# Finer order of norms and maxima, and the PSUM banks of the attentions split three to one

## The reference, cut to what matters

```
x = x + tanh(g_xattn[0]) * differential_attention(q=layernorm(x), k,v=ctx)   # 32 half heads of 8
x = x + tanh(g_ffn[0])   * zone_ffn(layernorm(x))                            # top 3 of 8 zones per sample
x = x + tanh(g_xattn[1]) * cross_attention(q=layernorm(x), k,v=ctx)          # 16 heads of 16
x = x + tanh(g_ffn[1])   * gated_ffn(layernorm(x))                           # silu(gate) * up, hidden 768

layernorm: (x - mean) / sqrt(var + 1e-5)
attention: softmax over the 77 context rows; differential: softmax_even - lam * softmax_odd
zone_ffn:  router from the mean over 1024 rows; sum of w_e * gelu(x @ Wa[e]) @ Wb[e]; plus x
```

## Time and profile before

| what | us |
|---|---|
| median of three runs (762.97 to 767.08) | 765.22 |
| the profiled execution, its own time | 768.97 |
| its span in the profile | 767.2 |
| PE busy in the span | 665.0 (87%) |
| DVE, ACT, POOL busy | 402.6, 337.8, 93.2 |
| mean granted TensorE clock | 0.899 |

### The profile page before, as it was taken

How to read it: one execution, slowest core, us unless ns; L and a number is a source line. 1 busy time by engine, 2 the same in 40 slices (tenths; PEclk the granted TensorE clock), 3 DMA queues, 4 the chain that set the end, 5 groups by cost and what they waited for, 6 DMA issues and landing times.

```text
span 767.2 us, 9986 instructions
## 1 busy us (share of the span) xinstructions
PE 665.0 (87%) x3644; PEld 496.5 (65%) x3644; DVE 402.6 (52%) x870; ACT 337.8 (44%) x555; POOL 93.2 (12%) x114
## 2 busy tenths in 40 slices
PE   1777886797888899999989999998887878999996
PEld 0545453453536778888867888876556666788885
DVE  6666755657677453333445635534445655444332
ACT  2221443454595474655635635543543344222232
POOL 4100123133363000000000000000021123000000
PEclk9956688879798999999999999999887569899999
DMA  6412011101021203030022150000162000000000
GB/s 195 88 25 69 1 43 45 39 25 25 3 84 53 85 1 111 0 110 1 4 107 69 42 165 3 0 1 3 38 171 61 24 3 1 1 1 27 29 29 27
DMA packets 22737, 34.66 MB, mean 45 GB/s; under 512 B 4640, under 2 KB 13216, under 8 KB 22688
## 3 DMA queue, kind: packets, MB, share of 16 engines
q1 hardware_dynamic: 21952, 33.66, 14.9%
q0 software_dynamic: 448, 0.29, 0.4%
q10 hardware_dynamic: 288, 0.07, 0.0%
HBM read 18.93 MB, written 2.10 MB: 27 GB/s over the span
## 4 chain that ended last, share of the span: by engine, by line
PE 74%; DVE 13%; issue 5%; ACT 3%; SPq 2%; POOL 2%; DMA 1%; ACTq 0%; DVEq 0%; POOLq 0%
PE SC L1084 27%; PE PV L1084 22%; PE AUX L1084 6%; PE AUX L1183 5%; PE PV L1102 5%; PE SC L1208 4%; PE AUX L1142 3%; DVE NM L972 3%; DVE XN L899 2%; DVE O L980 1%; DVE ST L879 1%; SPq L502 1%; POOL RSTD L571 1%; DVE QG L802 1%; PE AUX L1194 1%
## 5 line engine op out<-in xcount | busy, mean ns | idle before, releaser
L811 DVE TENSOR_TENSOR HL<-HF,HH 128x512 fp32r<-128x512 f32 x120 | 82.9, 690 | 153.5 <-ACT HH L762 153.2
L722 ACT ACTIVATE PB<-SC 77x1024 f32<-77x1024 f32 x96 | 94.6, 1015 | 73.5 <-PE SC L1208 73.2
L1183 PE MATMUL AUX<-KA,QG 96*128 96x308 f32 (+1 forms) x256 | 79.5, 385 | 37.3 <-DVE NM L972 26.6
L972 DVE TENSOR_REDUCE NM<-AUX 128x4 f32<-128x308 f32 x192 | 85.7, 468 | 38.5 <-PE AUX L1183 36.8
L1183 PEld LDWEIGHTS AUX<-KA,QG 96*128 96x128 f32 x256 | 53.4, 228 | 77.9 <-DVE NM L972 44.3
L762 ACT ACTIVATE HH<-PV 128x512 fp32r<-128x512 f32 x96 | 57.4, 597 | 73.3 <-PE SC L1084 73.2
L757 ACT ACTIVATE HF<-PV 128x512 f32<-128x512 f32 x96 | 57.4, 598 | 58.8 <-PE PV L1084 56.0
L1084 PE MATMUL PV<-XH,WAH 128*128 128x512 f32 x192 | 79.1, 412 | 1.8 <-DVE O L980 1.8
L1084 PE MATMUL PV<-XH,WAL 128*128 128x512 f32 x192 | 76.6, 399 | 0.0
L1084 PE MATMUL PV<-XL,WAH 128*128 128x512 f32 x192 | 76.6, 399 | 0.0
L1084 PE MATMUL SC<-HH,WBH 128*128 128x512 f32 x192 | 76.1, 396 | 0.0
(11 more groups left out here) (177 smaller groups left out, 1155.3 us busy)
## 6 DMA issues: line engine op xcount, KB each, us to landing
QG<-QH SPq DMA_DIRECT2D x128, 64.0 KB, 2.0
WSA<-in_wa SPq DMA_DIRECT2D x6, 1024.0 KB, 4.9
WSB<-in_wb SPq DMA_DIRECT2D x12, 512.0 KB, 6.9
QG<-QL SPq DMA_DIRECT2D x64, 64.0 KB, 2.0
X<-in_x SPq DMA_DIRECT2D x4, 512.0 KB, 6.0
out_x<-X SPq DMA_DIRECT2D x4, 512.0 KB, 2.7
WI<-in_wg SPq DMA_DIRECT2D x1, 768.0 KB, 5.4
WI<-in_wu SPq DMA_DIRECT2D x1, 768.0 KB, 8.8
```

The lines of the kernel that those rows point to most:

```text
L722: act.activation(probs(n)[0:S, :, :], SC[0:S, n % 2, :, :], ACT.Exp, scale=SCALE[a]).then_inc(exp_done, 1)
L811: return dve.tensor_tensor(dst, raw, hi.bitcast(F32), ALU.subtract)
L972: dve.tensor_reduce(NM[:, n % 2, t, 4 * u:4 * u + 4], bank(key)[:, 0:4 * S].rearrange("p (h n) -> p h n", h=4), AX_X, ALU.max, negate=True ...
L1183: ins = pe.matmul(ps[:, i * n_cols:(i + 1) * n_cols], QG[n % 2][0:ROWS, g, P * t:P * (t + 1)], KA[a][0:ROWS, j // 2, NS[a] * g:NS[a] * (g ...
```

## The change: what it does

1. **Norms**: `norm` becomes four `stats` steps and one `norm` step, placed in different gaps; `scale` is a step of its own in the plan, moved to ScalarE (four Identity activations with scale and bias); POOL makes one more small product for its bias. `residual` moves to POOL (two small and four 128x256 instructions).
2. **Maxima**: the heads' halves c = 0 and 1 are handed over apart: `negmax` of one half transposes half the heads, and SP issues 4 DMAs. Attends of the first half wait for the first hand-over only. Of tile 0, half 0 stays in the prologue; half 1 (16 maxima) becomes filler of attention tile 0.
3. **Keys** of the second attention become five steps inside attention tile 1, with the splits of its weights, whose low parts POOL makes (three instructions).
4. **Banks**: outside of zones and gated, one PV bank joins the AUX ring (three slots); `values` use the other bank alone and wait for the `outputs` just before.

```diff
+    def half_maxima(a, j, c):
+        half = units(a) // 2
+        return [("max", a, j, t, c * half + u) for t in range(TT) for u in range(half)] + [("negmax", a, j, c)]
+    def norm(stage, j):
+        return [("stats", stage, j, t) for t in range(TT)] + [("norm", stage, j)]
+    def norm_in(side, at, stage, j, gap, turn_gap):
+        for i, step in enumerate(norm(stage, j)):
+            side.setdefault(at + i // 2, []).append(step)
+        side.setdefault(at + 2 + gap, []).append(("scale", stage, j))
+        side.setdefault(at + 2 + gap + turn_gap, []).append(("turn", stage, j))
-    steps += [("keys", 0)]
-    steps += weave(maxima(0, 0), {3: [("norm", ATT0, 1)], 9: [("turn", ATT0, 1)],
-                                  13: [("query", 0, 1)] + moves(0, 1), 26: [("weights_split", 2)]})
-    steps += [("coefficients",), ("keys", 1)]
+    steps += keys(0, 0, 5) + [("heads", 0)]
+    steps += weave(half_maxima(0, 0, 0), {2: norm(ATT0, 1), 5: [("scale", ATT0, 1)], 8: [("turn", ATT0, 1)],
+                                          11: [("query", 0, 1)] + moves(0, 1)})
+    steps += [("coefficients",)]
...
+        if j == 0:
+            filler = half_maxima(0, 0, 1) + filler
+        if j == 1:
+            side.setdefault(1, []).append(("weights_split", 2))
+            for i, step in enumerate(keys(1, 0, 5)):
+                side.setdefault(6 + 2 * i, []).append(step)
         if j + 2 < J:
-            side.setdefault(1, []).append(("norm", ATT0, j + 2))
-            side.setdefault(3, []).append(("turn", ATT0, j + 2))
-            side.setdefault(6, []).append(("query", 0, j + 2))
+            norm_in(side, 0, ATT0, j + 2, 2, 2)
+            side.setdefault(8, []).append(("query", 0, j + 2))
         if j:
-            side.setdefault(7, []).append(("norm", FFN0, j - 1))
-            side.setdefault(11, []).append(("turn", FFN0, j - 1))
+            norm_in(side, 8, FFN0, j - 1, 2, 2)
-        steps += attention_tile(0, j, side, filler, 0, 12, left)
+        steps += attention_tile(0, j, side, filler, 0, 14 if j else 16, left)
...
-    side.setdefault(3, []).append(("norm", FFN0, 3))
-    side.setdefault(5, []).append(("turn", FFN0, 3))
-    side.setdefault(7, []).append(("residual", 3))
+    side.setdefault(1, []).extend(norm(FFN0, 3))
+    side.setdefault(3, []).append(("scale", FFN0, 3))
+    side.setdefault(5, []).extend([("turn", FFN0, 3), ("residual", 3)])
-    side.setdefault(b1 + 4, []).append(("norm", ATT1, 0))
-    side.setdefault(b1 + 6, []).append(("turn", ATT1, 0))
+    norm_in(side, b1 + 2, ATT1, 0, 1, 2)
+    norm_in(side, b1 + 8, ATT1, 1, 1, 2)
-    side.setdefault(b1 + 44, []).append(("norm", ATT1, 2))
-    side.setdefault(b1 + 46, []).append(("turn", ATT1, 2))
+    side.setdefault(b1 + 43, []).extend(norm(ATT1, 2))
+    side.setdefault(b1 + 45, []).append(("scale", ATT1, 2))
+    side.setdefault(b1 + 47, []).append(("turn", ATT1, 2))
...
-    steps += [("norm", FFN1, 2)]
-    side = {1: [("turn", FFN1, 2)], 3: [("turn_mix", 3)], 5: [("project", 3)], 6: [("norm", FFN1, 3)],
-            10: [("turn", FFN1, 3)]}
+    steps += norm(FFN1, 2)
+    side = {0: [("scale", FFN1, 2)], 1: [("turn", FFN1, 2)], 3: [("turn_mix", 3)], 5: [("project", 3)],
+            6: norm(FFN1, 3), 8: [("scale", FFN1, 3)], 10: [("turn", FFN1, 3)]}
...
+        if step[0] in ("zone", "gated"):
+            banks = 2
+        elif step == ("attend", 1, 0, 0):
+            banks = 3
         for key in slots_of(step):
             aux[key] = len(aux)
+            turn_now = (turn_now + 1) % banks
+            home[key] = (turn_now, uses[turn_now])
...
         def bank(key):
-            return AUX[:, aux[key] % 2, :]
+            n = home[key][0]
+            return AUX[:, n, :] if n < 2 else PV[:, 1, :]
@@ POOL @@
                     pool.tensor_tensor(RSTD[:, 1, :], RSTD[:, 0, :], NHALF[:, :], ALU.pow).then_inc(pool_step, 1)
                     chain += 1
                     pool.wait_ge(pool_step, chain)
+                    pool.tensor_tensor(RSTD[:, 3, :], RSTD[:, 2, :], RSTD[:, 1, :], ALU.mult).then_inc(rstd_ready, 1)
+                elif kind == "residual":
...
                     for t in range(TT):
+                        xt = X[:, TT * j + t, :]
+                        ins = pool.tensor_scalar(xt, xt, AB[:, 0, t:t + 1], AB[:, 1, t:t + 1], ALU.mult, ALU.add)
...
+                elif kind == "weights_split" and step[1] == 2:
+                    pool.wait_ge(split_hi, 5)
+                    lo_part(WQ1L[:, :, :], WQ1R[:, :, :], WQ1H[:, :, :]).then_inc(split1_done, 1)
+                    pool.wait_ge(split_hi, 6)
+                    for c in range(KC):
+                        lo_part(WDL[:, c, :, :, :], ...
@@ ACT @@
+                elif kind == "scale":
+                    _, stage, j = step
+                    n = order[step]
+                    act.wait_ge(rstd_ready, n + 1)
+                    if n:
+                        filled(act, ("turn",) + NORMS[n - 1][1:] + (KC - 1,))
+                    for t in range(TT):
+                        ins = act.activation(XN[:, t, :], X[:, TT * j + t, :], ident_f, scale=RSTD[:, 1, t:t + 1],
+                                             bias=RSTD[:, 3, t:t + 1])
@@ PE @@
-                if q >= 2:
-                    pe.wait_ge(pv_out, q - 1)
+                if q >= 1:
+                    pe.wait_ge(pv_out, q)
...
-                            ins = pe.matmul(PV[32 * r:32 * r + DV + 1, q % 2, at_h:...
+                            ins = pe.matmul(PV[32 * r:32 * r + DV + 1, 0, at_h:...
...
-                    if u == 0:
-                        pe.wait_ge(m_moved[m % 2], 16 * G * (m // 2 + 1))
+                    if u % (units[a] // KC) == 0:
+                        pe.wait_ge(m_moved[m % 2][u // (units[a] // KC)], 16 * (G // KC) * (m // 2 + 1))
```

More of the change, by code:

```diff
@@ L52 @@
 SMALL = 13
-SCALE_LAG = 3
 LAG = 2
@@ L223, in plan @@
     steps += [("gated_end",), ("evac", FFN1, 3), ("out", FFN1, 3)]
-    placed, waiting = [], []
-    for step in steps:
-        if waiting and (step == ("turn",) + waiting[0][1:] or waiting[1] == 0):
-            placed.append(waiting[0])
-            waiting = []
-        placed.append(step)
-        if step[0] == "norm":
-            waiting = [("scale",) + step[1:], SCALE_LAG]
-        elif waiting:
-            waiting[1] -= 1
-    return placed
+    return steps
 def slots_of(step):
@@ L863, in _ @@
                     lo_part(WVL[:, :, :], WVR[:, :, :], WVH[:, :, :]).then_inc(split_done, 1)
+                elif kind == "stats":
+                    _, stage, j, t = step
+                    if t == 0:
+                        if stage == ATT0:
+                            dve.wait_ge(x_in[j], 16)
+                        elif stage == FFN0:
+                            dve.wait_ge(mixed, oct_of(0, j + 1, 0))
+                        else:
+                            for i in range(2):
+                                used(dve, ("out", FFN0, j, i) if stage == ATT1 else ("project", j, i))
+                    ins = dve.bn_stats(ST[:, t, :], X[:, TT * j + t, :])
+                    if t == TT - 1:
+                        ins.then_inc(stats_done, 1)
                 elif kind == "norm":
@@ new lines, in _ @@
+                elif kind == "keys" and step[2] < 3:
+                    _, a, i = step
+                    low = slice(64, ROWS)
+                    key = step + (0,)
+                    groups = range(3 * i, min(3 * i + 3, G))
+                    dve.wait_ge(keys_hi, 3 * a + i + 1)
+                    if a == 0:
+                        kt = KT[0][low, groups[0]:groups[-1] + 1, :]
+                        ins = lo_part(kt, bank(key)[low, 0:len(groups) * B * S].rearrange("p (g n) -> p g n", n=B * S), kt)
+                    else:
+                        for g in groups:
+                            kt = KT[1][low, g, :]
+                            at_g = (g - 3 * i) * B * S
+                            ins = dve.scalar_tensor_tensor(kt, bank(key)[low, at_g:at_g + B * S], BQD[low, g:g + 1],
+                                                           kt.bitcast(F32), ALU.add, ALU.subtract)
+                    ins.then_inc(frees(key), 1)
+                elif kind == "keys":
+                    _, a, i = step
+                    key = step + (0,)
+                    if i == 3:
+                        dve.wait_ge(pool_set, 5)
+                        if a == 1:
+                            dve.wait_ge(small_in, 16 * SMALL)
+                    filled(dve, key)
+                    v = V[a][0:S, i - 3, :, 0:DV]
+                    ps = bank(key)[0:S, 0:D].rearrange("p (h d) -> p h d", d=DV)
@@ L968, in _ @@
                     key = step + (0,)
[L969 to L970 removed]
+                    half = units[a] // 4
+                    if t == 0 and u % half == 0 and n >= 2:
+                        filled(dve, ("negmax", (n - 2) // J, (n - 2) % J, u // half, 0))
                     filled(dve, key)
```

281 lines of the change are left out of this document (117 added, 164 removed).

## The result

The changed kernel took 742.8 us, median of four runs (732.87 to 744.41), the kernel before beside it 764.1: ratio 0.964, 95% interval 0.953 to 0.976. The forecast was 745. Six more runs on another occasion had a median of 738.7 (732.6 to 749.2), ratio 0.965 (0.9605 to 0.970). The profiled run after took 744.27 us, the one before 768.97: 24.7 apart.

What follows compares the result with a forecast made beforehand. The prediction took TensorE, busy 87% of the span, to bound the kernel, so gains had to come from its waits or clock. Terms by stretch, plus the clock, summed to -20.4 from 765.2: 745 us, range 725 to 759.

Steps and rivals of the forecast that it cites:

- Prologue, -6: Before the first attend: work leaves, but SP's query moves ahead of the maxima's DMAs limit the gain to 6 us.
- The ring, two thirds of its waits: Attention tiles 0 to 2: a third AUX bank removes two thirds of the 16.4 us that maxima's matmuls wait.
- Tile 0, +1.9: First attention's tile 0: 16 maxima added, +7.4; DMA stop, ring waits and norm block saved; net 1.9 us longer.
- Tile 1, +0.9: First attention's tile 1: five keys steps cost 6 us, ring waits save 4.8, with smaller terms; net 0.9 us longer.
- Tile 2, -3.8: First attention's tile 2: ring waits -3.4, DMA and norm block -1.4, negmax +1; net 3.8 us shorter.
- Tile 3, +3: First attention's tile 3: ScalarE's extra instructions and the single values bank cost, the moved residual saves; net 3 us longer.
- Clock, -4: Attention tiles 0 to 2: fewer stops raise TensorE's granted clock, saving 4 us; bounds +4 to -18.
- Zones, -6.7: Zones: turns stand further from their norms, so three waits for XN, 8.1 us, go; net 6.7 us shorter.
- D: Rival, chance 0.08: `values` steps wait for transpositions in the single values bank; 24 us or more, 769 us and above.
- A: Rival, chance 0.20: the clock comes back, tiles 0 to 2 run at 0.95; 730 us.
- B: Rival, chance 0.16: finer order makes new waits, the ring saves one third, the clock nothing; 756 us.
- C: Rival, chance 0.06: zones and gated keep their waits in another place, scale standing behind gelus on ScalarE; no change.

Runs made afterwards that it cites:

- e3: The changed kernel with tile 1's 24 query moves placed behind the maxima's four DMAs of tile 0's first half; 732.3 us, ratio 0.960.
- e1: The kernel before with only the ring of three banks and one bank for the values; 753.6 us, ratio 0.984.
- e2: The changed kernel without its ring: two AUX banks and two banks for the values; 762.8 us, ratio 0.9957.
- e4: The changed kernel with the second attention's weight split and keys back ahead of the first attend; 722.2 us, ratio 0.944.
- the second profile: Another profiled run of the changed kernel, nothing changed, also called "again"; 737.92 us.
- e8: The changed kernel with the ring's third bank given back to the values in tile 3 of the first attention; 737.3 us, ratio 0.962.
- e10: The changed kernel with keys and earlier split before the first attend, moves later, two values banks in tile 3, route later, XN on VectorE; 709.8 us, ratio 0.930.
- e11: As e10, but XN written by ScalarE as in the changed kernel; 716.2 us, ratio 0.935.
- e7: The changed kernel with the second attention's split and keys ahead of the first attend and tile 1's query moves behind the maxima's DMAs; 727.5 us, ratio 0.948.

## Why the prediction was right

**Prologue, -6: right, and for its reason** (-6.6). SP's queue was full from 51.06 until the maxima's DMAs, TensorE idle before the attend, and e3 moved it to 60.0 by SP's order alone.

**The ring, two thirds of its waits: right in the number, but not the ring's alone.** 16.4 us became 5.0. The ring alone took off 4.9 (e1), the finer order alone 8.5 (e2), and the ring on top of it 2.9. The forecast had given all of it to the ring, and had e2 too fast for that reason.

**Tile 0, +1.9: measured -4.6 and -2.8.** What failed is that the sum had no clock of its own here. Half-clock surcharge fell from 6.5 to 1.1 and 2.9 us, stops from 10.6 to 6.6.

**Tile 1, +0.9: measured -3.1, yet its largest term was wrong.** "Woven they cost little more than their matmuls, 6": e4 put the keys at 13.2. Other savings, the ring's above all (e1's tile 1 is 5.6 us shorter than before), hid this. It is the most costly miss, since the 15 us hole that I had forecast in the prologue was the place for these steps.

**Tile 2, -3.8: measured -0.1 and -0.8.** The change itself put a stop here that I had not seen. Before, the turn whose parts the route reads stood 4.7 us ahead of the route's first matmul, with attends and `values` between, and that matmul waited for nothing; now the turn is the step just ahead. Timelines of PE, before and after:

```profile
199.98 2.00 PE L1142 MATMUL AUX<-ident,XN 128*128 128x128 f32 x8
...
204.68 0.63 PE L1223 MATMUL AUX<-POOLED,W 128*64 128x1 f32 x8
```

```profile
185.18 1.04 PE L1164 MATMUL AUX<-ident,XN 128*128 128x128 f32 x8
189.07 0.60 PE L1249 MATMUL PV<-POOLED,W 128*64 128x1 f32 x8 [2.85 <-DVE XL L850]
```

The half clock did not shrink in this tile either (3.8 us before, 4.8 and 3.3 after).

**Tile 3, +3: measured +10.6 and +3.9.** Of the second profile's 3.9 us 2.6 are half clock, and 1.3 are left for ScalarE, outputs and bank, which I had at 3. For the half clock I had no term here, because the earlier trace rows shows 0.93. There is one profile of the kernel before, and none of the thirteen others has more than 0.86 here, so that may have been one run's draw; it may also be the change.

**Clock, -4: inside its range for tiles 0 to 2, at half of what was measured, and wrong in place.** The surcharge of tiles 0 to 2 fell by 8.3 (8.0 again), tile 3's rose by 10.5 (2.6), and the second attention's fell by 11.2 (10.5), where I had nothing. There the stops did not shrink (28.5 to 29.9 us), so most of the second attention's -8.9 is the clock. How much of it is chance, e3 shows, which has the same steps there as the changed kernel:

```profile
514.20:613.50 99.30, 80.71 (x792) 62.99 (x790) 52.43 (x109) 53.36 (x67) 20.56 (x17) 0.78 0.21 57
```

At 0.78, near the 0.75 of before, it took 99.3 us, 2.1 less than before; at 0.87 the changed kernel took 92.5, at 0.92 e8 took 89.5. What raised the clock there stays open: e1, the ring alone, has 0.80, and e2, all but the ring, 0.82. Of my terms the ring's -2.8 was near (the maxima's waits for a reduction went from 4.2 to 2.1), and the second hand-over's +0.9 too small (its waits for the last reduction went from 3.7 to 7.7).

**Zones, -6.7: measured -6.5** (-8.7 in e8 and e10, at clock 1.00). **Gated, -2.8: measured -5.6**, half of it the clock (surcharge 2.8 to 0).

The sum of forecasts was -20.4 and of measurements -24.7, and -31.0 in the second profile, where tile 3 had less half clock. It came out close because tile 3's half clock paid for the gains in tiles 0, 1 and the second attention: right in direction, in the mechanism of prologue, zones and gated, and in the total partly by luck. Of the rivals, D (the single bank) cost 3.5 us in tile 3 (2.7 in the second profile) and never 24; A's clock came back in part here, and wholly (1.00) only in tiles 0 and 1 of e4 and 0 to 2 of e10; of B's new waits one was seen, at the route in tile 2, and C's not.

## What to carry to other kernels

When a change empties a stretch of TensorE, look at once for what can be put there, and at what stands ahead of the releasing DMA on its queue, and see that a step that needs another's result is not moved right behind it: here keys and moves, with a bank and an engine put back, gave as much again as the change itself. Give a woven step its price in the bank that it holds and in the clock, not only its matmuls. And compare stretches of several profiles before a stretch's clock becomes a term of a sum.

## What the runs showed of the hardware

TensorE stayed at 1.2 GHz for 28 us in which the profile shows it busy without a gap (192 to 220), in a mix of attends and of `values` matmuls of 77 rows and 17 columns out, and likewise from 170 to 194 in e10 and e11. The same program left this state at other times in other runs (tile 3 of 29.5 against 36.2 us). With 12 matmuls of 128x512 in a row at this place the clock was at 2.4 GHz within 5 us in two kernels, in one of them no sooner than without them.

The Trainium skill, "TensorE: Matmul & The Clock Gate", section "A second HAM failure mode: psum-queue depth-cycling", puts a swinging clock down to small idle times at the banks. The runs agree in part: with ring waits cut by two thirds tile 0 rose from 0.80 to 0.96 and 0.89. Against it stand tile 3, which has no such waits and the lowest clock of all, 0.59, and tiles 0 to 2 of e10, which have 7.3 us of them where the changed kernel has 5.0, at 1.00.

POOL took 3.58 us for the two instructions that write the low parts of a weight in three copies (from 57.49 in e7), and with the split right ahead of the keys TensorE stood 6.22 us for them; with the split one query earlier it did not stand at all.
